# A new order of the work on every engine in the first experts stage of an audio tower, with router, gates and second normalisation moved

## What is computed

```python
def _L0_ffn_ref(x, gate_w, gate_b, w1, b1, w2, b2, gamma, beta):
    gate_logits = x @ gate_w + gate_b                       # 16 experts
    topk_vals, topk_idx = jax.lax.top_k(gate_logits, 2)
    topk_w = jax.nn.softmax(topk_vals, axis=-1)
    h = jax.nn.relu(jnp.einsum('bsh,ehf->bsef', x, w1) + b1)
    expert_out = jnp.einsum('bsef,efh->bseh', h, w2) + b2
    sel = jnp.take_along_axis(expert_out, topk_idx[:, :, :, None], axis=2)
    y = x + jnp.sum(topk_w[..., None] * sel, axis=2)
    return (y - mean(y)) / jnp.sqrt(var(y) + EPS) * gamma + beta

h = h + _L0_ffn_ref(_layernorm(h), ...)
```

## Time and profile before

| | us |
|---|---|
| median of 3 runs | 1213.65 (1213.61 to 1213.88) |
| the profiled execution | 1214.44 |
| its span in the profile | 1212.7 |
| TensorE busy | 1053.4 (87%) |
| VectorE, ScalarE, GpSimd busy | 724.5, 690.5, 508.0 |
| first and last start of a product with the gates (L1454) | 427.5 and 786.8 |
| mean granted TensorE clock over the span | 0.939 |

### The profile page before, as it was taken

The page is one execution under the profiler, slowest core; times in us unless marked ns, Lnnn a source line. Parts: engine busy times, 40 slices in busy tenths (PEclk is TensorE's granted clock), DMA queues, the critical chain, the costliest instruction groups (busy, mean ns, idle before and its releaser), DMA issues.

```text
span 1212.7 us, 35394 instructions
## 1 busy us (share of the span) xinstructions
PE 1053.4 (87%) x12426; PEld 733.9 (61%) x12426; DVE 724.5 (60%) x1976; ACT 690.5 (57%) x1290; POOL 508.0 (42%) x780
## 2 busy tenths in 40 slices
PE   3698865999998798888888889969999999968998
PEld 1254444777766676666677667736666666645555
DVE  3466634677745646555655655627888888863443
ACT  1245443777754565565556556537777777744554
POOL 0000002555526455555555555534555555542110
PEclk9999986999977999899899989969999999988999
DMA  9423000000000000000000000000000000000101
GB/s 250 67 38 42 1 1 0 2 0 0 0 1 1 1 2 3 2 0 0 0 0 0 0 0 1 3 1 1 3 0 0 0 0 0 1 1 10 22 17 22
DMA packets 10769, 14.92 MB, mean 12 GB/s; under 512 B 9296, under 2 KB 9296, under 8 KB 9680
## 3 DMA queue, kind: packets, MB, share of 16 engines
q1 hardware_dynamic: 10704, 14.06, 5.5%
HBM read 11.96 MB, written 2.10 MB: 12 GB/s over the span
## 4 chain that ended last, share of the span: by engine, by line
PE 70%; DVE 10%; issue 10%; ACT 4%; POOL 4%; DVEq 1%; DMA 0%; ACTq 0%; SPq 0%; POOLq 0%
PE ps L1332 7%; PE ps L1320 7%; PE ps L1701 6%; PE ps L1723 5%; PE ps L1709 4%; PE ps L221 3%; PE ps L1691 3%; PE ps L1865 3%; PE ps L1898 3%; POOL e_acc L1282 3%; PE ps L1689 2%; PE ps L859 2%; PE ps L858 2%; PE ps L231 2%; DVE c_max L351 2%
## 5 line engine op out<-in xcount | busy, mean ns | idle before, releaser
L1496 ACT ACTIVATE e_hid<-ps,cst 128x512 f32<-128x512 f32 x256 | 161.3, 680 | 101.8 <-PE ps L1320 101.6
L1332 PE MATMUL ps<-ew,e_hid 128*64 128x64 f32 x4096 | 155.5, 230 | 41.1 <-ACT e_hid L1496 40.8
L1332 PEld LDWEIGHTS ps<-ew,e_hid 128*64 128x64 f32 x4096 | 136.2, 141 | 78.4 <-ACT e_hid L1496 48.3
L1282 POOL TENSOR_TENSOR e_acc<-e_acc,e_part 128x512 f32<-128x512 f32 x96 | 125.3, 1306 | 107.6 <-DVE e_part L1454 107.2
L1320 PE MATMUL ps<-e_xs,ew 64*128 64x256 f32 x1024 | 153.6, 428 | 0.0
L1454 DVE TENSOR_TENSOR e_part<-ps,e_wt 128x512 f32<-128x512 f32 x128 | 88.1, 688 | 99.0 <-PE ps L1332 95.9
L1320 PEld LDWEIGHTS ps<-e_xs,ew 64*128 64x128 f32 x1024 | 98.4, 204 | 19.7 <-issue 3.5
L1747 DVE TENSOR_REDUCE a_rmax<-ps 128x8 f32<-128x1024 f32 x64 | 78.2, 1223 | 36.0 <-PE ps L1701 34.0
L1656 POOL TENSOR_TENSOR a_sum<-a_part 128x256 f32<-128x256 f32 x64 | 46.5, 726 | 105.1 <-DVE a_part L1758 105.1
L1709 PEld LDWEIGHTS ps<-cst,a_ex 128*128 128x128 f32 x512 | 55.0, 140 | 49.7 <-issue 49.7
L204 POOL TENSOR_TENSOR t_prob<-t_ex,t_rscale 128x512 f32<-128x512 f32 x8 | 12.0, 1502 | 169.4 <-DVE t_rscale L377 169.4
(11 more groups left out here) (272 smaller groups left out, 2207.4 us busy)
## 6 DMA issues: line engine op xcount, KB each, us to landing
x_in<-x_dram SPq DMA_DIRECT2D x48, 128.0 KB, 4.7
cst<-cst_dram SPq DMA_DIRECT2D x1, 2965.0 KB, 16.6
out_dram<-e_res SPq DMA_DIRECT2D x16, 128.0 KB, 2.0
ew<-ew_dram SPq DMA_DIRECT2D x1, 1024.0 KB, 18.6
cst<-cst_dram SPq DMA_DIRECT2D x1, 704.0 KB, 7.5
ew<-ew_dram SPq DMA_DIRECT2D x1, 512.0 KB, 20.3
cst<-cst_dram SPq DMA_DIRECT2D x1, 329.5 KB, 3.1
```

The lines of the kernel that those rows point to most:

```text
L1282: eng.tensor_tensor(acc[:, :, :, :], acc[:, :, :, :], part[n % RING][:, :, :, :], ALU.add).then_inc(sum_sb.sem, 1)
L1332: mm = eng.matmul(m.ps[rows, 6 + n % 2, to:to + C], hid[e % 4][:, a:a + C], w2[:, e * C:e * C + C], start=True, stop=True)
L1496: nc.scalar.activation(hid[e % 4][:, :].rearrange("p (r t) -> p r t", r=2), m.ps[:, 2 + 2 * (n % 2):4 + 2 * (n % 2), j * 256:(j + 1) * 256 ...
```

## The change

The same work is put in another order on all four engines, in one function per piece. What differs in what is executed:

- The router weights stand in the constants as `gatebd`, 128 rows by 32 columns with zeros off the diagonal blocks, so that two products per group (all 128 rows, 32 columns) take the place of eight. All logits lie in bank 0.
- The multiplication by gamma is made by POOL (`scale`) instead of DVE, with a semaphore `yg_sb` of its own.

What moves:

- PE: hidden(0) of the next group ahead of out(7); the transposes of the gates and the next group's turn behind out(0); logits of the next group behind out(1); biases behind out(2). The waits of hidden(0), hidden(1), out(0) and out(1) ask for fewer of the previous group's steps.
- ACT: the copies `xs` of the next group and `wT` behind ReLU 3, the exponential behind ReLU 9, the square root of the previous group behind ReLU 13.
- DVE: `y` of the previous group (`sums`) and the next group's logits and maxima (`best`) behind product 1, the gap, indices and masks (`choose`) and the statistics of `y` behind product 2, `base` and the variance behind product 3, `soften` behind product 5. Scaling, addition into `h` and statistics of `h` are those of the group two back, behind products 0, 4 and 6. The gap is taken ahead of the indices.
- POOL: beta of the next group first; gamma (two back) behind add 1; centring (one back) behind add 4; the first normalisation of the group two ahead behind add 5; the gates of the next group behind add 6.

The diff, cut to its core:

```diff
-COLS += [("gatew", EXPERTS0), ("gatebr", EXPERTS0), ("iota16", EXPERTS0), ("eb1", EXPERTS0),
+COLS += [("gatebd", 2 * EXPERTS0), ("gatebr", EXPERTS0), ("iota16", EXPERTS0), ("eb1", EXPERTS0),
...
+    def rounds(eng, rest, tail=None):
+        rest(0, 0, 0, 2)
+        rest(1, 1, 1, 2)
         with eng.Fori(1, TG // 2 - 1) as i:
-            rest(2 * i, 0, call(ahead, 2 * i + 1, 1), call(finish, 2 * i - 1, 1))
-            rest(2 * i + 1, 1, call(ahead, 2 * i + 2, 0), call(finish, 2 * i, 0))
-        rest(TG - 2, 0, call(ahead, TG - 1, 1), call(finish, TG - 3, 1))
-        rest(TG - 1, 1, call(None, 0, 0), call(finish, TG - 2, 0))
-        for k in range(E if finish else 0):
-            finish(TG - 1, 1, k)
+            rest(2 * i, 0, 2, 2)
+            rest(2 * i + 1, 1, 2, 2)
+        rest(TG - 2, 0, 2, 1)
+        rest(TG - 1, 1, 2, 0)
+        if tail:
+            tail(TG - 1, 1)
...
+        def scale(g):
+            eng.wait_ge(yn_sb.sem, yn_sb.at(g))
+            eng.tensor_tensor(yn[:, :, :], yn[:, :, :], col(m, "gamr").unsqueeze(1).broadcast_to(ALL),
+                              ALU.mult).then_inc(yg_sb.sem, 1)
...
+        def rest(g, b, back, more):
+            if more:
+                beta(g + 1)
+            add(g, 1)
+            if back > 1:
+                scale(g - 2)
+            add(g, 2)
+            add(g, 3)
+            add(g, 4)
+            if back:
+                centre(g - 1)
+            add(g, 5)
+            if more > 1:
+                eng.wait_ge(base_sb.sem, base_sb.at(g))
+                T.pool(eng, g + 2, b)
+            add(g, 6)
+            if more:
+                weigh(g + 1, 1 - b)
+            add(g, 7)
             eng.wait_ge(sum_sb.sem, sum_sb.at(g, NE - 1))
             eng.wait_ge(y_sb.sem, y_sb.at(g - 1))
             eng.tensor_tensor(fold[:, :, :], acc[:, :, 0, :], acc[:, :, 1, :], ALU.add).then_inc(sum_sb.sem, 1)
+        def tail(g, b):
+            scale(g - 1)
+            centre(g)
+            scale(g)
         eng.wait_ge(*T.norm)
         eng.memset(wT[:, :], 0.0).then_inc(zeros, 1)
-        rounds(eng, rest, ahead, finish)
+        T.pool(eng, 0, 0)
+        T.pool(eng, 1, 1)
+        weigh(0, 0)
+        beta(0)
+        rounds(eng, rest, tail)
...
+        def turn(g, b):
+            eng.wait_ge(logit_sb.sem, logit_sb.at(g - 1))
+            T.pe(eng, g, b)
...
         def logits(g, b):
             eng.wait_ge(T.xs_sb.sem, T.xs_sb.at(g))
             for p in range(TS // 2):
+                mm = eng.matmul(m.ps[:, 0, 256 + 2 * p * E:256 + 2 * (p + 1) * E], T.xs[b][:, p * P:(p + 1) * P],
+                                col(m, "gatebd"), start=True, stop=True)
+            mm.then_inc(logit_ps.sem, 1)
...
+        def hidden(g, b, n):
+            if n == 0:
+                eng.wait_ge(T.xs_sb.sem, T.xs_sb.at(g))
+            eng.wait_ge(hid_sb.sem, hid_sb.at(g, 2 * n - 2) if n >= 2 else hid_sb.at(g - 1, E - 2 + 2 * n))
...
+        def out(g, b, n):
+            eng.wait_ge(part_sb.sem, part_sb.at(g, n - 1) if n >= 2 else part_sb.at(g - 1, NE - 1 + n))
...
+        def turn_weights(g, b):
+            eng.wait_ge(wt_sb.sem, wt_sb.at(g))
+            eng.wait_ge(base_sb.sem, base_sb.at(g - 1))
...
+        def rest(g, b, back, more):
             for n in range(NE):
                 if n + 1 < NE:
...
+                    hidden(g, b, n + 1)
+                elif more:
+                    hidden(g + 1, 1 - b, 0)
+                out(g, b, n)
+                if n == 0:
+                    turn_weights(g, b)
+                    if more:
+                        turn(g + 1, 1 - b)
+                if n == 1 and more:
+                    logits(g + 1, 1 - b)
+                if n == 2:
+                    biases(g)
...
+        T.pe(eng, 0, 0)
+        logits(0, 0)
+        hidden(0, 0, 0)
+        rounds(eng, rest)
...
+        def normal(g):
+            eng.wait_ge(dev_sb.sem, dev_sb.at(g))
+            eng.reciprocal(y_rstd[:, :], y_dev[:, :]).then_inc(rstd_sb.sem, 1)
+            eng.wait_ge(yc_sb.sem, yc_sb.at(g))
+            eng.wait_ge(rstd_sb.sem, rstd_sb.at(g))
+            eng.wait_ge(h_sb.sem, h_sb.at(g - 1))
+            eng.tensor_tensor(yn[:, :, :], yc[:, :, :], bc(y_rstd[:, :], ALL), ALU.mult).then_inc(yn_sb.sem, 1)
...
+        def best(g):
             eng.wait_ge(logit_ps.sem, logit_ps.at(g))
-            eng.tensor_tensor(logit[:, :, :].rearrange("p (a r) e -> p a r e", r=2),
-                              m.ps[:, 0:2, 256:256 + 2 * E].rearrange("p r (a e) -> p a r e", a=2),
-                              col(m, "gatebr").unsqueeze(1).unsqueeze(1).broadcast_to([P, 2, 2, E]),
-                              ALU.add).then_inc(logit_sb.sem, 1)
+            eng.tensor_tensor(logit[:, :, :], m.ps[:, 0, 256:256 + TS * E].rearrange("p (s e) -> p s e", s=TS),
+                              col(m, "gatebr").unsqueeze(1).broadcast_to([P, TS, E]), ALU.add).then_inc(logit_sb.sem, 1)
             eng.wait_ge(logit_sb.sem, logit_sb.at(g))
-            eng.wait_ge(gap_sb.sem, gap_sb.at(g - 1))
             settle(eng, m)
...
+        def choose(g):
             eng.wait_ge(top_sb.sem, top_sb.at(g))
             settle(eng, m)
+            eng.wait_ge(gexp_sb.sem, gexp_sb.at(g - 1))
+            eng.tensor_tensor(gap[:, :], top[:, :, 1], top[:, :, 0], ALU.subtract).then_inc(gap_sb.sem, 1)
             for s in range(TS):
...
+        def weighted(g, b, n):
+            if n == 0:
+                eng.wait_ge(wt_sb.sem, wt_sb.at(g))
+            eng.wait_ge(out_ps.sem, out_ps.at(g, n + 1))
+            eng.wait_ge(sum_sb.sem, sum_sb.at(g, max(n - RING, 1)) if n >= RING else sum_sb.at(g - 1, min(NE - 2 + n, NE - 1)))
...
+        def rest(g, b, back, more):
+            for n in range(NE):
+                weighted(g, b, n)
+                if n == 0 and back > 1:
+                    normal(g - 2)
+                if n == 1:
+                    if back:
+                        sums(g - 1)
+                    if more:
+                        best(g + 1)
+                if n == 2:
+                    if more:
+                        choose(g + 1)
+                    if back:
+                        count_y(g - 1)
+                if n == 3:
+                    bias(g, b)
+                    if back:
+                        variance(g - 1)
+                if n == 4 and back > 1:
+                    result(g - 2)
+                if n == 5 and more:
+                    soften(g + 1)
+                if n == 6 and back > 1:
+                    count(g - 2)
+        def tail(g, b):
+            sums(g)
+            normal(g - 1)
+            count_y(g)
+            result(g - 1)
+            variance(g)
+            count(g - 1)
+            normal(g)
+            result(g)
+            count(g)
+        best(0)
+        choose(0)
+        soften(0)
+        rounds(eng, rest, tail)
...
+        def rest(g, b, back, more):
...
+                relu(g, e)
+                if e == 3:
+                    if more:
+                        T.act(eng, g + 1, 1 - b, hid_ps)
+                    turned(g)
+                if e == 9 and more:
+                    exp(g + 1)
+                if e == 13 and back:
+                    deviation(g - 1)
+        def tail(g, b):
+            deviation(g)
         eng.preload_act_table(ACT.Exp)
-        rounds(eng, rest, ahead, finish)
+        T.act(eng, 0, 0, hid_ps)
+        exp(0)
+        rounds(eng, rest, tail)
...
-    twice("gatew", f0("gate_w")), rows("gatebr", f0("gate_b"))
+    for s in range(2):
+        gate = np.zeros((C, 2, EXPERTS0), np.float32)
+        gate[:, s, :] = f0("gate_w")
+        put("gatebd", gate, 64 * s)
+    rows("gatebr", f0("gate_b"))
```

More of the change, by code:

```diff
@@ new lines, in out @@
+        def out(g, b, n):
+            eng.wait_ge(part_sb.sem, part_sb.at(g, n - 1) if n >= 2 else part_sb.at(g - 1, NE - 1 + n))
+            for j in range(2):
+                e = 2 * n + j
+                eng.wait_ge(hid_sb.sem, hid_sb.at(g, e + 1))
+                for s in range(TS):
+                    for rows in HALVES:
+                        a, to = place(s) * P + rows.start, (2 * s + j) * C
+                        mm = eng.matmul(m.ps[rows, 6 + n % 2, to:to + C], hid[e % 4][:, a:a + C],
+                                        w2[:, e * C:e * C + C], start=True, stop=True)
+            mm.then_inc(out_ps.sem, 1)
@@ new lines, in turn_weights, with biases @@
+        def turn_weights(g, b):
+            eng.wait_ge(wt_sb.sem, wt_sb.at(g))
+            eng.wait_ge(base_sb.sem, base_sb.at(g - 1))
+            for s in range(TS):
+                mm = eng.transpose(m.ps[0:E, 1, s * P:(s + 1) * P], wt[b][:, s, :], col(m, "ident"))
+            mm.then_inc(wT_ps.sem, 1)
+        def biases(g):
+            eng.wait_ge(wT_sb.sem, wT_sb.at(g))
+            for s in range(TS):
+                for rows in HALVES:
+                    a = s * P + rows.start
```

(3 more changed lines are left out.)

282 lines of the change are left out of this document (89 added, 193 removed).

## The result

The changed kernel takes 1159.8 us, the median of 4 runs (1155.98 to 1160.62); the kernel before, run beside it, takes 1213.77. The ratio is 0.9541 with an interval of [0.9511, 0.9571], so it is **faster by 54.0 us**; the forecast was 53.0. The profiled execution took 1160.27.

A forecast was written before the change was run, and what follows sets the result against it. TensorE was taken to be held by ReLUs queued behind ScalarE's waits and table loads, and by lost clock. -63.6 + 9.8 - 0.5 + 1.3 = -53.0 us from 1213.65 gave 1160.7 us, range 1148 to 1177.

The forecast's parts named there:

- case A: First experts stage: TensorE sets the pace, the gates' weights cost it 0.2 to 1.2 us a group; 1153 to 1167, chance 0.52.
- Base, -63.6: TensorE over 15 groups: 18.72 us per group if nothing stalls, 280.8 instead of 344.4, so 63.6 us less.
- The stall at the gates, +9.8: TensorE's gate transposes wait for GpSimd's weighting, 0.75 us in each of 13 groups: 9.8 us back, bounds 0 and 15.6.
- far end: Upper bound of the gate transposes' wait: 1.2 us per group, 15.6 us, if VectorE and GpSimd exclude each other.
- ScalarE's loads covered: ScalarE: exponential behind ReLU 9 and square root behind ReLU 13 have both table loads covered by 0.7 us.
- VectorE: Gives up gamma, otherwise same work in other places, about 14 of 18.7 us; no out(n) waits.
- Prologue, -0.5: Before the stage: the eight logits at the low clock, 1.04 us busy, shrink to about half, 0.5 us less.
- Tail, +1.3: Stage end: two normalisations open instead of one, with gamma on GpSimd in the chain: 1.3 us more, bounds 0 and 2.5.
- B: No stall at all, as the engines' exclusion falls between other operations: sum -62.8, 1151; chance 0.22.
- C: Second wait: ReLUs behind table loads late, or GpSimd's delay reaches next group's products 0 and 1; 1166 to 1190, chance 0.19.
- D: Gates' weights so late that TensorE stands over 2.7 us per group and its clock falls: about 1230, chance 0.03.
- E: Exponential still waits for the gap because `best` waits for the second sum: near 1205, chance 0.04.

The follow-up runs named there:

- gates ahead of add 6: Changed kernel with GpSimd's weighting of the gates put in front of its add 6 instead of behind it: 1156.58 us, repeated at 1153.26 us.
- hidden(0) behind out(7): Changed kernel with the next group's hidden(0) on TensorE put back behind out(7), as in the kernel before: 1161.49 us.
- before without the second table: Kernel before with the second normalisation's deviation by an exponential instead of a square root, so no table loads in the stage: 1186.61 us.
- router late: Changed kernel with `best` and `choose` behind product 5, `soften` behind product 6, and exponential and square root exchanging places: 1175.36 us.
- before, router early: Kernel before with only the router moved: two-product logits ahead of out(3), gap ahead of the indices, exponential two ReLUs earlier: 1193.5 us.
- before, router early, root late: Kernel before with the router's work earlier and the square root behind ReLU 7 instead of 4, its following steps two later: 1169.84 us.
- the same, sum later too: Kernel before with earlier router, `y` and its statistics moved into the next group, square root behind ReLU 9, and the changed kernel's finer waits: 1177.14 us.

## Why the prediction was right

The forecast, case A, holds: 1159.8 against 1160.7, in A's own span of 1153 to 1167, with all of its signs but one, for the logits take 0.57 us and not 0.3. But two of its terms were mis-sized, and their errors had opposite signs.

**Base, -63.6: -60.2.** A group without a stall takes 18.95 us, not 18.72: from 427.51 to 465.41 two groups pass without one, 18.95 each. The step that failed is "the nearest row is the turn, also two products". The logits start at 603.69 and the hidden products behind them at 604.26: 0.57, where I took 0.28. One such product of the source is two instructions in the trace, while each of the turn's two transposes is one: four products of the source were the x8 of the earlier trace rows, and two are x4. The "eight" was a count of instructions and the "two" a count of products, so "two of the eight" was no case at all. Each of the four costs twice as much as each of the eight. The upper bound, no gain, was right; that is 15 x 0.29 = 4.3 us, of which the other parts give 0.9 back. Whether the new form earns its place otherwise is open. All logits lie in bank 0, so the router can be read before `base`; the old one lies in bank 1 too, from which `base` reads. The old form in the new order wasn't tried.

**The stall at the gates, +9.8: +2.7.** Place and releaser are as forecast, its size is not: 286.99 - 15 x 18.95 = 2.7 us, about 0.2 in each of 12 groups, the low end of A. The weights are ready at 619.85, 21.44 us behind the start of hidden(1) (617.60 less a group), between my 20.6 and 22.1. What failed is the choice of 0.75, "nearer to the far end because the order makes the collision regular". It is regular, but which operation pays is set by which starts first. The variance starts 0.17 behind add 3 and pays 0.97 us, near enough what I charged. The addition into h starts 0.16 ahead of add 4 and keeps its short form; add 4 takes 1.38 us instead of 1.26, where I had let it wait the full 0.43. The chain behind it had errors both ways. Add 5 starts at 615.02, 16.6 us into the group, where I had 15.3 at best: product 4 stood behind the variance, and behind add 4 stands the centring of 0.6 us, which my chain left out. From there to the weights it is 4.83 us; my four terms add up to 5.05, and 20.6 less 15.3 is 5.3, so the 0.2 of waiting was counted twice. That the whole stall hangs on GpSimd's order is shown by the gates ahead of add 6 (stage -2.5 and -3.0).

The Trainium skill (SBUF — State Buffer, section "SBUF: two separate sides") says that the two engines take one port pair by turns and that the later one blocks fully. The variance agrees to 0.03 us. Add 4 agrees less well: it starts with 0.25 us of the addition still to come and is stretched by 0.12. By the rule the far end, 15.6, was to hold; measured it is 2.7, because the second collision and the chain came out smaller.

**ScalarE's loads covered: right.** The changed kernel without them has the same stage to 0.01 us. The cover of 0.7 us at out(7) is measured as 0.72, and hidden(0) behind out(7) confirms it from the other side.

**VectorE: right in that no out(n) waits.** The cast of the indices, which falls beside add 2, pays 0.6 us of exclusion too; I had not priced it, and no product of TensorE waits for it. **Prologue, -0.5: 0.** From the turn's start to out(0) of group 0 it is 5.62 us and was 5.61: the logits last 0.99 there (423.02 to 424.01) where the eight had 0.85, by the same mis-count. **Tail, +1.3: +1.55** (last product's end to the statistics' end: 9.65, was 8.10), with both waits for gamma on GpSimd in it.

**The sum.** Base and prologue came out 3.9 us dearer than forecast and the stall 7.1 cheaper, the tail 0.25 dearer: -55.95 us in the stage instead of -53.0. The stages outside it, in which nothing was to change, took 1.7 back. That the median lies within 1 us of the forecast is luck in part: before and before without the second table differ in nothing ahead of the stage, and their stages begin at 426.22 and 422.42 us.

**The rivals.** B, no stall, was out by 0.2 us a group, closer than my own 0.75; it is what the gates' version reaches. C did not come, but two edits of the changed kernel made it: 0.4 us at out(7) with hidden(0) behind it, 1.4 with the router late. D would have needed the clock to fall, and E the gap to be late; the clock is 1.00 and the gap not waited for.

**Where the 55.9 us of the stage came from.** TensorE's busy and idle time over the stage, from one window of each profile (us; idle is stage less busy):

| kernel | stage | busy | idle |
|---|---|---|---|
| before | 368.6 | 323.6 | 45.0 |
| before, router early | 346.7 | 306.8 | 39.9 |
| before, no second table | 338.9 | 309.9 | 29.0 |
| before, router early, root late | 323.0 | 302.9 | 20.1 |
| the same, sum later too | 331.4 | 305.1 | 26.3 |
| after | 312.7 | 306.9 | 5.7 |
| after, router late | 330.0 | 308.9 | 21.1 |
| after, gates ahead of add 6 | 310.2 | 306.4 | 3.8 |

All but the first have about the same busy time, 14 to 21 us less than it: every edit tried that shortens the longest idle time gets the clock back, 16.7 us in the changed kernel. My base mixed this with the idle time. The other 39.2 are idle time, and no single part has them: the early router alone takes 5 of them, with the late square root 25. Undone by itself in the new order, the router costs 15 us of idle time. The parts don't add, since each stall shadows the next: gap, variance, fold, `xn`. Three runs in a row (router early; with it the root late; with these the sum late) each removed one and showed the next. How the last 10.3 us of the stage (323.0 to 312.7) divide between the earlier `xn`, the finer waits and the later `y` was not separated.

## What to carry to other kernels

When an engine waits in order for a late input, list what stands behind that wait on every other engine before moving it: removing the first one brought two fifths of the gain here, most of it clock, and the next wait took the rest. Look for the instruction that is cheap but queued behind a dear one (three short operations behind an add of 1.3 us), and let the producer run one or two rounds ahead rather than merely earlier. Where two engines exclude each other, lay the starts against each other, for here the later one paid nearly all.

## What the runs showed of the hardware

- **Very small operations pay the full exclusion.** Subtracting 4 elements per partition took 1.12 us beside GpSimd's add instead of 0.16. The cast of 8 elements shows the same (the one at 607.90 ends at 608.67, add 2 at 608.64), min/median/max in the kernel after:

```profile
L1449 DVE CAST e_idxf<-e_idx x16: 172/762/766, 425.8 to 703.7; 128x8 f32<-128x8 uint32 x16
```

- **The clock held through idle times of up to 1.73 us per group in one kernel and 2.03 in another** (no second table, and router early: 1.00 over 250 us in both) and fell behind one of 2.68. So the kernel before paid twice for its longest stall, and each of the two one-part edits took the second payment away.
- **A table load takes ScalarE its own length and no more here.** The exponential starts 1.30 us behind the start of the load at 609.33, the square root 1.30 behind the one at 613.62. The Trainium skill (ScalarE: Activation LUTs, section "What ACT_TABLE_LOAD costs") adds a drain of some 1380 ns to the load; no row here shows one, and the measurement decides.
- **A product over 128 rows with 32 columns is no cheaper than two over 64 rows with 16.** Four instructions of the first kind take 0.57 us, eight of the second 0.55.
